# Moving three kinds of work by a few units in the hand-written order of a decoder kernel

## The reference

```
x = layernorm(x + attention(x))            # 16 query heads on 4 key/value heads, over the axis of length 4
x = layernorm(x + ssm(ctx, gate=x))        # state space model: 16 states, 512 channels, scan over 512 steps
x = layernorm(x + ffn(x))                  # weights looked up in a table of 16 values
...
def step(state, xs):
    d_t, B_t, C_t, u_t = xs
    dA = jnp.exp(d_t[..., None] * A)
    state = state * dA + (d_t * u_t)[..., None] * B_t[:, None, :]
    y_t = jnp.einsum('ben,bn->be', state, C_t)
    return (state, y_t)
```

## Time and profile before

| | |
|---|---|
| median of 3 runs | 1080.19 us (1077.92 to 1082.95) |
| the profiled execution | 1080.77 us, its span 1079.0 us |
| PE busy | 856.7 us (79%) |
| DVE busy | 790.1 us (73%) |
| ACT busy | 695.9 us (64%) |
| POOL busy | 587.0 us (54%) |
| granted TensorE clock, mean | 0.862 |
| L802 on POOL, 256 products | 363.0 us busy, 78.1 idle before them |
| L708 on DVE, 256 scans | 295.8 us busy, 69.4 idle before them |
| software DMA queue (POOL's) | 67.11 MB, 32.9% of 16 engines' span |
| hardware DMA queue (SP's) | 78.53 MB, 21.7% |

### The profile page before, as it was taken

How to read it: one execution, slowest core, us unless ns; L and a number is a source line. 1 busy time by engine, 2 the same in 40 slices (tenths; PEclk the granted TensorE clock), 3 DMA queues, 4 the chain that set the end, 5 groups by cost and what they waited for, 6 DMA issues and landing times. The chain is left out here.

```text
span 1079.0 us, 12490 instructions
## 1 busy us (share of the span) xinstructions
PE 856.7 (79%) x3752; PEld 626.2 (58%) x3752; DVE 790.1 (73%) x1248; ACT 695.9 (64%) x1078; POOL 587.0 (54%) x563
## 2 busy tenths in 40 slices
PE   5858798797787977868650346899999999989997
PEld 2536654475445754455430235687778787768886
DVE  3577898887978779867861477769999999445543
ACT  3387994789747997568850556557777787333331
POOL 0048965898659986599893443325555455100000
PEclk8888978898888879879665677899999999989999
DMA  7035986799978998779998822111111111132321
GB/s 242 31 117 137 225 177 176 159 258 223 208 162 175 223 229 199 137 174 229 217 242 171 320 79 98 60 30 50 39 42 55 39 49 29 39 81 67 116 75 52
DMA packets 53686, 146.49 MB, mean 136 GB/s; under 512 B 5684, under 2 KB 14004, under 8 KB 43908
## 3 DMA queue, kind: packets, MB, share of 16 engines
q0 software_dynamic: 9216, 67.11, 32.9%
q1 hardware_dynamic: 43056, 78.53, 21.7%
q10 hardware_dynamic: 1364, 0.25, 0.1%
HBM read 58.97 MB, written 91.10 MB: 139 GB/s over the span
## 5 line engine op out<-in xcount | busy, mean ns | idle before, releaser
L802 POOL TENSOR_TENSOR state<-state,crep 128x512 f32<-128x512 f32 x256 | 363.0, 1794 | 78.1 <-DVE state L708 78.0
L708 DVE TENSOR_TENSOR_SCAN state<-decay,banks 128x512 f32<-128x512 f32 x256 | 295.8, 1202 | 69.4 <-PE banks L412 45.7
L1060 PE MATMUL banks<-x2T,wgu 128*128 128x512 f32 x1056 | 251.1, 400 | 8.8 <-POOL wgu L1365 8.8
L412 PE MATMUL banks<-ident,scaled 128*128 128x128 f32 x1024 | 181.2, 322 | 69.4 <-DVE state L708 51.8
L1060 PEld LDWEIGHTS banks<-x2T,wgu 128*128 128x128 f32 x1056 | 203.4, 193 | 55.7 <-issue 12.5
L545 ACT ACTIVATE decay<-delta,negA 128x512 f32<-128x512 f32 x256 | 170.3, 719 | 80.8 <-DVE state L708 80.3
L412 PEld LDWEIGHTS banks<-ident,scaled 128*128 128x128 f32 x1024 | 137.7, 164 | 139.4 <-DVE state L708 59.1
L534 ACT ACTIVATE scaled<-duT,BT 128x512 f32<-128x512 f32 x256 | 163.5, 717 | 9.9 <-DVE duT L685 9.8
L1148 ACT ACTIVATE leaf<-bit,table,table_gap 128x512 f32<-128x512 int32 x198 | 149.5, 807 | 17.2 <-DVE w L1242 17.1
L1242 DVE COPY_PREDICATED leaf<-bits,leaf 128x512 f32<-128x512 int32 x132 | 120.1, 926 | 14.9 <-issue 13.7
L1354 POOL TENSOR_TENSOR pool_wait_here<-minus_half 128x1 f32<-128x1 f32 x33 | 8.6, 262 | 159.5 <-DVE w L1242 145.7
(11 more groups left out here) (113 smaller groups left out, 1197.1 us busy)
## 6 DMA issues: line engine op xcount, KB each, us to landing
y_scratch<-state POOLq DMA_DIRECT2D x60, 1024.0 KB, 9.0
crep<-c_scratch SPq DMA_DIRECT2D x64, 256.0 KB, 5.5
idx_sb<-in_idx SPq DMA_DIRECT2D x33, 256.0 KB, 2.8
xT_sb<-in_xT SPq DMA_DIRECT2D x16, 256.0 KB, 4.7
x_sb<-in_x SPq DMA_DIRECT2D x4, 1024.0 KB, 7.8
y_scratch<-u SPq DMA_DIRECT2D x4, 1024.0 KB, 6.2
y_scratch<-state SPq DMA_DIRECT2D x4, 1024.0 KB, 6.7
x_scratch<-x_sb SPq DMA_DIRECT2D x4, 1024.0 KB, 6.5
```

Source lines behind the costliest of these rows:

```text
L412: last = nc.tensor.transpose(banks[:, k % NB, lc * LQ:(lc + 1) * LQ], scaled[:, g % SR, lc, et * P:(et + 1) * P], ident[:])
L708: V.tensor_tensor_scan(state[:, g % GR, et, :], decay[:, k % DR_RING, :], banks[:, k % NB, :], 0.0, ALU.mult, ALU.add).then_inc(scan_ready, 1)
L802: G.tensor_tensor(state[:, g % GR, et, :], state[:, g % GR, et, :], crep[:, g % CR, :], ALU.mult)\
L1060: last = mm(banks[:, 2 * tb + w, :], wgu[:, par, w, ws, t * P:(t + 1) * P], x2T[:, xs, t, tb * 512:(tb + 1) * 512], start=t == 0 and n == ...
```

## The change

On PE the transposes of attention move from units (2, 0) and (2, 1) to (3, 0) and (3, 1) in rows 0 to 2, and in row 3 by one to three units. In row 3 the projections move by one unit. On DVE the residuals stand later in every row, on POOL the norm factors two units later ((15, 2) for (15, 0)), and on ACT the norm's application moves from the end of slot 15 into slot 0 of the next row, before the copies of the input projection; ACT's `keep_attT` stand one slot later. On SP the store of `x_sb` and the load into it stand one slot later.

```diff
-        ATT_AT = {(2, 0): 3, (2, 1): 0, (4, 1): 2, (6, 0): 1}
-        LAST_ATT_AT = {(2, 1): 3, (2, 2): 0, (3, 2): 2, (4, 3): 1}
+        ATT_AT = {(3, 0): 3, (3, 1): 0, (4, 1): 2, (6, 0): 1}
+        LAST_ATT_AT = {(3, 0): 3, (3, 1): 0, (4, 0): 2, (5, 0): 1}
         att_nth = ATT_ORDER.index
         PROJ_AT = {(14, 1): 3, (14, 2): 2, (14, 3): 1, (15, 0): 0}
-        LAST_PROJ_AT = {(5, 0): 3, (5, 2): 2, (6, 0): 1, (6, 2): 0}
+        LAST_PROJ_AT = {(5, 1): 3, (5, 3): 2, (6, 1): 1, (6, 3): 0}
...
-                        if n == 2 and b:
+                        if n == 3 and b:
                             store_x1(b - 1)
                         if n == 2 and b + 2 < S:
                             load_ctx(b + 2)
-                        if n == 4 and b:
+                        if n == 5 and b:
                             load_x(b)
...
-                        if n == 1:
+                        if n == 0 and b:
+                            normalized(b - 1)
+                        if n == 2:
                             keep_attT(b, 3)
                             keep_attT(b, 0)
-                        elif n == (4 if more else 2):
+                        elif n == (4 if more else 3):
                             keep_attT(b, 2)
-                        elif n == (5 if more else 3):
+                        elif n == (5 if more else 4):
                             keep_attT(b, 1)
...
-                            elif n == 15:
-                                normalized(b)
...
-                RES_AT = {(13, 3): 3, (14, 0): 2, (14, 1): 1, (14, 3): 0}
-                LAST_RES_AT = {(5, 1): 3, (5, 3): 2, (6, 1): 1, (6, 3): 0}
+                RES_AT = {(14, 1): 3, (14, 2): 2, (15, 0): 1, (15, 1): 0}
+                LAST_RES_AT = {(5, 2): 3, (6, 0): 2, (6, 2): 1, (7, 0): 0}
...
-                            if at == ((15, 0) if more else (7, 0)):
+                            if at == ((15, 2) if more else (7, 1)):
                                 norm_factors(b)
```

## The result

The changed kernel took 1088.97 us (median of 19 runs, 1084.92 to 1096.38), the kernel before 1081.75 us (19 runs, 1077.92 to 1085.38) on the same chips. The ratio is **1.0076 (95% interval 1.0062 to 1.0091)**, that is +8.2 us where the prediction had +4.4. The profiled execution of after took 1088.1 us with a span of 1086.3 us, beside 1080.77 and 1079.0 before.

What follows compares the result with a forecast made beforehand. Bound by POOL, its DMA queue, then DVE in row 1, and POOL in row 3. Row 0 +0.3, row 1 +0.5 + 1.5, row 2 +0.5 + 2.2, row 3 -2.7 + 2.1: +4.4, median 1084.5 us, range 1076 to 1091.

Steps and rivals of the forecast that it cites:

- End of a row: Rows 0 to 2: reordered scans, residuals and norm factors gain DVE 1.7 us and POOL 2.7 us.
- The norm's application on ACT: Slot 0: moved behind the scaling, it lets `keep_in` begin 1.6 us earlier, and DVE's taps with it.
- Attention's transposes: PE, rows 1 and 2: about 6.2 us at half clock hold POOL's product; 1.6 us gained become 0.5 us lost per row.
- Row 0: No store or load; later attention transposes delay scan (3, 1) and ACT's silu: +0.3 us, between 0 and 0.7.
- The late load's traffic in rows 1 and 2: SP's load falls wholly into POOL's busy time: 1.5 us extra in row 1, 2.2 in row 2.
- The store, "no cost": SP's store of `x_sb` moves into 222 to 230 us, where POOL's queue has nothing to serve: no cost.
- The first residual of row 3: It waits for x, issued about 495.8, landing near 504.5; POOL has until about 508 us, so no cost.
- its own test: Among its conditions, the forecast is wrong if the first residual of row 3 holds DVE past 508 us.
- the -2.7 of row 3's sum: POOL, the bound of row 3, keeps its 2.7 us gain from the row's start; the load adds 2.1.
- Rival 3: Load served at the sums' pace, at the knots of 253.09 and 516.99: +12.5 us, 1092.7 us; chance 0.22.
- Rivals 1 and 2: Load absorbed: -1.4, 1078.8 us, chance 0.17 (with rival 4); also attention at full clock: -5.9, 1074.3 us, chance 0.13.
- The rule weighed in the prediction: About 2.0 us plus bytes by 436 GB/s, 4.4 us for 1 MB: POOL's queue would never back up, moved load free.

Runs made afterwards that it cites:

- att_back: `store_load_back` with attention's transposes of rows 0 to 2 back behind units (2, 0) and (2, 1), ACT's copies back in slot 1; 1074.33 us, 0.9937 of before.
- row3_load_back: Changed kernel with the load of x back in slot 4 in row 3 alone, rows 1 and 2 keeping slot 5; 1082.5 us, 1.0000 of before.
- load_back: Changed kernel with SP's load of x back in slot 4, all else of the change kept; 1079.85 us, 0.9976 of before.
- load_late_alone: Kernel before with one edit, the load of x in slot 5 for slot 4; 1099.18 us, 1.0157 of before.
- store_load_back: Changed kernel with both SP's store of x_sb back in slot 2 and the load back in slot 4; 1075.35 us, 0.9945 of before.

## Why the prediction came out as it did

The direction and the order of size were right, but the total owes this to luck, to errors of opposite sign: the sum had +4.7 us for rows 1 and 2 and -0.6 for row 3, the trace has +0.7 and +9.1. By the prediction's own steps:

- **End of a row: right where it was worked out, at the end of row 0.** Scan (15, 2), forecast for 194.3, begins the run of six at 191.34, 3.0 us earlier; POOL's factors, forecast for 196.8 to 198.8, run from 193.98 to 195.94, 2.8 to 2.9 us earlier. The kernel was 2.9 us ahead by then (132.5 to 129.6 at row 0's softplus), so the steps themselves hold to 0.1 us. DVE's first wait for the projections fell from 2.94 to 0.76 us in row 0, as said (under 1), and to 1.10 and 1.08 us in rows 1 and 2. DVE and POOL of after, end of row 0:

```profile
191.34 6.75 DVE L708 TENSOR_TENSOR_SCAN state<-decay,banks 128x512 f32<-128x512 f32 x6
```

```profile
193.98 0.23 POOL L824 TENSOR_SCALAR vareps<-meanvar 128x4 f32<-128x4 f32 x1
...
195.94 2.50 POOL L802 TENSOR_TENSOR state<-state,crep 128x512 f32<-128x512 f32 x2
```

- **The norm's application on ACT: right.** It stands behind slot 0's scaling and decays, and `keep_in` follows it at once. `keep_in` begins at 202.03 where it began at 206.56: 4.5 us earlier, of which 2.9 came in with row 0 and the start, so 1.6 of its own, the figure forecast.

```profile
199.21 2.92 ACT L522 ACTIVATE x_sb<-x_sb,shift,rstd 128x512 f32<-128x512 f32 x4
202.03 2.76 ACT L442 ACTIVATE conv_in<-banks,ch 128x512 f32<-128x512 f32 x4
```

- **Attention's transposes: mechanism right, size wrong.** The clock is neither that of before nor full: 0.80 in their stretch, 4.5 us instead of 6.2. The four short bursts of transposes, one each 3.3 us, had looked to me like rest. POOL waited 0.63 us, not 2.0, and the issue that was to come 0.5 us later came 1.0 us earlier. This took most of the forecast loss off rows 1 and 2, which came out 4 us better. By `att_back` the whole move is worth nothing that shows. Row 0, given +0.3, came out at -1.1: there too the transposes took less (4.78 us at 87.28) than the 6.20 before, but at this size I don't call it shown.

- **The late load's traffic in rows 1 and 2: within its bounds.** Sum of 3.7 us forecast for both rows, with bounds of 0 and 9.1. The closest test is `row3_load_back` against `load_back`, 2.6 us by the ratios; by the pieces `load_late_alone` shows 4.8, `load_back` against after 0.9. The knot's wait grew by 1.1 us in row 1, near the 1.5.

- **The store, "no cost": wrong beside the load's old place, untested beside the new one.** With the load in its old place the late store costs about 0.3%. The prediction read POOL's queue as empty from 222 to 230 us; in before it served 80 packets there, 0.52 MB, all but one of them by 226. More than that, SP's own queue wasn't empty: the store goes beside the odd sum and takes 9.1 us for 6.1, and in `load_back` the load must wait for it. The failed step was to price a moved transfer by one queue alone, and not to ask what has to wait for its landing.

- **The first residual of row 3: the step that failed.** The prediction had the load "issued at about 495.8" (it was 494.87) and landing "near 504.5". That gave it 8.7 us, near the 7.3 to 7.9 us of its old places in before; it landed at 514.6, 19.7 us behind its issue. In its old place in row 3, issued at 490.67, it took 7.3 us, and POOL's queue had 33 packets served beside 690 of SP's from 491 to 498 us. In its new one POOL's queue takes 89.1% of the engines' time from 502 to 508 us, and the 16.1 us of a sum in the earlier trace rows gave notice that nothing lands quickly there. The prediction named the right place and the point (508 us), and its own test says it failed: the residual held DVE to 514.64. POOL's idle times in row 3 up to its sum at 582.64 (575.74 in before) come to 15.2 us, the 11.65 among them, and to 4.9 us in before, most of it the 3.88 of the earlier trace rows, which is gone. That is 10.4 us more. Ahead of it POOL had won 1.1 us: the sum issued at 490.61 stands 81.2 us behind the last softplus, and 82.3 in before (493.93). The difference, 9.3, is the 9.1 of the piece but for 0.2. So the -2.7 of row 3's sum was mis-sized as well.

- **The rivals.** Rival 3 had the mechanism nearest to the truth (a load that is served worse beside sums), but its price was the sums' delay, at the knots; the real price was the load's own delay, at its reader. Its total of +12.5 us was about as far off as the forecast's +4.4, on the other side. Rivals 1 and 2 fall with row 3.

- **The rule weighed in the prediction.** The Trainium skill, "DMA: Bandwidth & Descriptors", Anatomy of one DMA, would give an estimate of 4.4 us for the megabyte of a sum; the trace has 17.4 us for the sum issued at 496.71 in after and 16.3 for one at 505 to 506 in before. A sum with none ahead of it in POOL's queue, issued at 493.93 in before, took 9.1 us. The trace doesn't agree, as said.

**What stays open.** Without the moved store and load the rest of the change gains 0.55%, 5.9 us (`store_load_back`), where the forecast's terms without the load's come to -1.4. The pieces of its one profile hold 4.2 us of it: 1.0 in row 0, 2.3 in the two middle rows, 0.9 in the last. How it splits between the residuals' and the norm's move wasn't tried. Nor is it settled why POOL has won 1.1 us and not 2.7 in the first groups of row 3, and nothing there in `load_back` (its issue at 493.41 is 82.7 us behind the last softplus).

## What to carry to other kernels

A moved DMA has two prices: what it does to the traffic around it, and its own time to landing in the company that it gets. Read the second from a transfer in the new stretch, not from its own row in the old one, and then go to its nearest reader and ask what is queued there; here that reader was a residual in front of all scans, and 19.7 us for 7.3 cost more than all other parts won. Here a load of larger pieces (of other rows of x), or a later reader, took back about the same 0.75% as the load at its old place in that row. And look at what must have landed before the transfer may start: with the load in its old place, a store moved one group later held up the load of the same buffer by 4.1 us.

## What was not expected of the hardware

Two DMA queues that both have work were served in turns, packet by packet, not byte by byte: 151 packets of POOL's queue and 159 of SP's in 6 us, with 1.11 and 0.32 MB, and with pieces of 8 KB on both sides 33 and 33 in 2 us, with 0.27 and 0.26 MB. A 1 MB load in 2 KB pieces went from 7.3 us (6.1 to 6.3 with POOL's queue nearly idle) to 19.7; in 8 KB pieces it took 11.8. The Trainium skill, "DMA: Bandwidth & Descriptors", Queues, rings and completion order, says that each DMA engine round-robins between the queue rows at packet granularity. The equal packet counts agree, but the start of the load doesn't show turns (3 packets of SP's queue beside 0.63 MB of POOL's in 3 us); what a page's packet holds and what one of the trace holds may differ, and no run here shows that.

TensorE's granted clock rose from 0.50 to 0.80 across two neighbouring stretches in which it had worked 1.99 of 5.30 us and then 4.60 of 4.60. Before the change, after 5.08 us of idle time, the same 32 transposes ran at 0.55 and took 6.4 us; now, after bursts of 1.1 us every 3.3 us, 4.5 us.
